# An attention and feed-forward kernel: x's layer norm and both its half-precision parts move to earlier stages, the router and the weights' pieces to later ones

## Chip, cores and metric

One Trainium2 chip, and of it one core. The metric is the device time of one launch in microseconds (us), the median of several runs.

## What is computed

The reference takes x (16 sequences, 256 channels, 1024 positions, float32) and a context y (16 x 256 x 512). Cut to what matters:

```python
xn = layernorm(x)                              # over the 1024 positions
q = ws(wq) @ y + bq;  k = ws(wk) @ y + bk      # ws: rows of the weights standardised
v = ws(wv) @ xn + bv
s = softmax(q @ k.T / SCALE)                   # 8 heads, 32 x 32 each
o = ws(wo) @ (s @ v) + bo + xn                 # then a norm over channels, gamma, beta, mask
x = x + tanh(g_xattn) * norm(o)
xr = layernorm(x).reshape(4096, 1024)          # tokens are the channels' rows
gates = top-2 of softmax(xr @ wr.T)            # 8 experts
h = silu(xr @ w1.T);  h = silu(h @ w3.T);  h = h @ w2.T
out = zeros; out[index of expert k] += gates[:, k] * h      # rows 0 to 7 only
x = x + tanh(g_ffn) * out
```

## The kernel before

Every float32 product is made of half-precision parts: a tensor is split into a high part (float16) and a low part (what the high one left out), and three products hi x hi, hi x lo, lo x hi are summed.

The 16 sequences go in 8 **pairs** (q = 2j and 2j + 1 for pair j; b is the place in the pair, 0 or 1). A pair's feed-forward part has 16 **groups** (g = 0 to 15): in each, TensorE makes eight steps (d = 0 to 7) of three products 128x128 by 128x512 (`ffn`, L665). Groups 0 to 7 multiply by w1, groups 8 to 15 by w3. In the same program order stand the 15 **stages** of the next pair's attention: stage s is mixed into group s + 1 of the pair before it. So pair j's feed-forward runs with pair j + 1's attention, and the kernel is one prologue (pair 0's attention and the split of the weights), eight pairs, and a short end. Groups and stages are written by hand in the same order on every engine; each engine has its own queue, runs it strictly in order, and waits on semaphores. What stands behind a waiting instruction waits too.

TensorE fills banks of PSUM. For a group g: ScalarE takes tanh (L899, `th_ready`), VectorE finishes the activation (L1344), ScalarE writes its high part (L905, `h_hi`), VectorE its low part (L1349, `h_lo`). Group g + 2 of TensorE needs L1344 of group g.

The steps of the attention that the text speaks of, by stage:

- Stages 0 and 2: four `project` products each (L539) on TensorE, emptied by VectorE (`qk_out`, L1292) and scaled by ScalarE (`q_scaled`, L842).
- Stages 1 and 3: `scores` (L548); VectorE's `softmax` (L1202 to L1218) with ScalarE's exponential (`score_exp`, L847) in its middle.
- Stages 3 and 4, d = 4: `out_times_scores` (L558). ScalarE writes its high part (`t1_high`, L858), VectorE its low part (`t1_low`, L1297).
- Stage 4, d = 0 and stage 5, d = 2: `times_value` (L573, L580), which needs `t1_low`. ScalarE empties it with `m_high` (L851 and, for cb, L854), VectorE with `m_low` (L1191). For b = 1, `out_times_scores` waits for the cb of b = 0 (`cb_evac`), since both use one bank.
- x's first norm: VectorE's statistics (`ln1`, L1176 and L1182), GpSimd's coefficients (`coefs`, L369 to L381, into `co`), ScalarE's `normed` (L793, writes xs), VectorE's high part (`x_high`, L1187), GpSimd's low part (`x_low`, L396). Stages 3 to 6.
- GpSimd's `bias_part` (L432) writes a part of the tile u, to which VectorE's `bias_tiles` (L1227) adds the rest.
- Stages 7 and 8, one per d: `long_product` (L595, L599), which needs x's high and low part; VectorE adds it to u (`attention_out`, L1243 and L1247, with statistics) and from its fifth tile on TensorE waits for VectorE to have emptied the bank.
- GpSimd's `add_beta` (L412, L415) and `values` (coefficients from the statistics of u); ScalarE's `v_normed` (L864); then TensorE's `attention_back` (L612) in stages 9 and 10.

The router (64 small products, L674, then `top_two` and `gates` on VectorE) is placed by three group numbers: its products behind group ROUTER[0], `top_two` behind group ROUTER[1], `gates` ahead of the activation of group ROUTER[2]. Its result is first needed in group 10.

In pair 0 the weights are still being split: a piece i (0 to 7 of w1, 8 to 15 of w3) is `w_high` on ScalarE (L831), `w_low` on VectorE (L1156) and two transposing DMAs from SyncE's queue (`turn`, L293). The pieces pass through five slots of buffers, and a slot is free when its last piece is turned. Group 8 of pair 0 needs all pieces of w3. In the tables below, names of buffers have their numbers left out (t_hi is t1_hi; h_hi and h_lo are also the slots of the weights' pieces).

Of the kernel before, what the change touches and what calls it, by code (L numbers as in the profile page):

```python
# [59 lines left out]
ROUTER = (1, 2, 3)  # L60
# [7 lines left out]
def build(nc, a, out):  # L68
# [14 lines left out]
    def w_slot(i):  # L83

        return ((3, 0), (4, 0), (0, 0), (1, 0), (2, 0), (0, 1), (1, 1), (2, 1),
                (0, 2), (1, 2), (2, 2), (0, 3), (1, 3), (2, 3), (0, 4), (0, 5))[i]

    def w_blocks(g):

        return {0: (5, 6, 7), 1: (8, 9), 2: (10, 11), 3: (12, 13), 4: (14,), 6: (15,)}.get(g, ())  # L90
# [5 lines left out]
    with ctx:  # L96
# [70 lines left out]
        co = sb("co", [P, 4, 2])  # L167
# [48 lines left out]
            mcur_set ln1_stat ln1_mv ln1_var ln1_rstd ln1_coef xs_ready xhi_ready xlo_ready mtmp_step xpre_ready  # L216
# [39 lines left out]
        def _(sp):  # L256
# [39 lines left out]
            def pair(j, last=False):  # L296

                load_x(j)
                if j == 1:
                    for i in range(FT, 2 * FT):  # L300
                        turn(i)
                if not last:
                    for b in range(2):
                        load_y(j + 1, b)
                store(j)
                for b in range(2):
                    tokens(j, b)
                if not last:
                    for b in range(2):
                        load_mask(j + 1, b)  # L310
# [18 lines left out]
            for i in range(2, FT):  # L329
                turn(i)  # L330
# [17 lines left out]
        def _(pool):  # L348
# [40 lines left out]
            def ln1(q):  # L389
                coefs(q, mv, co, CH, EPS, XS, "ln1", (sm["xs_ready"], q))  # L390

            def x_low(q, b):
                pool.wait_ge(sm["xhi_ready"], q + 1)
                for h in range(4):
                    n, at = h // 2, slice(TC * (h % 2), TC * (h % 2) + TC)
                    ins = pool.tensor_tensor(x_lo[:, b, n, at], xs[b][:, n, at], x_hi[:, b, n, at], ALU.subtract)  # L396
                ins.then_inc(sm["xlo_ready"], 1)
# [38 lines left out]
            def attention(j, s, jn=None):  # L436
                if s == 12 and jn is not None:
                    y_largest(jn)
                if s in (3, 4):
                    ln1(2 * j + s - 3)  # L440
                if s in (2, 3):
                    bias_part(2 * j + s - 2, s - 2)
                if s in (5, 6):
                    x_low(2 * j + s - 5, s - 5)
                if s == 7:
                    add_beta(j, 0, 0)
                    values(2 * j, 0)
                    add_beta(j, 0, 1)
                    add_beta(j, 1, 0)
                if s == 8:  # L450
                    values(2 * j + 1, 1)
                    add_beta(j, 1, 1)
                if s in (9, 10):
                    second_norm(2 * j + s - 9)
# [4 lines left out]
            ln1(0)  # L459
            x_low(0, 0)  # L460
            ln1(1)
# [18 lines left out]
        def _(pe):  # L480
# [154 lines left out]
            def ffn(j, g, d):  # L635
# [18 lines left out]
                else:  # L654
                    if g == FT:
                        pe.wait_ge(sm["h_lo"], GROUPS * j + d + 1)
                    if g == FT and d == 0 and first_pair(j):
                        for slot, n in enumerate((6, 4, 4)):
                            pe.wait_ge(w_turned[slot], 32 * n)
# [129 lines left out]
        def _(act):  # L789
            def normed(q, b, c_, s_coef, s_done):  # L790
                act.wait_ge(s_coef, q + 1)
                for c in range(CH):
                    ins = act.activation(xs[b][:, c, :], xa[b][:, c, :], ACT.Identity,  # L793
                                         bias=c_[:, 3, c:c + 1], scale=c_[:, 2, c:c + 1])
                ins.then_inc(s_done, 1)
# [93 lines left out]
            def attention_late(j, s, jn=None):  # L889
# [3 lines left out]
                if s in (4, 5):  # L893
                    normed(2 * j + s - 4, s - 4, co, sm["ln1_coef"], sm["xs_ready"])
# [17 lines left out]
            def group(j, g, ja=None, w3=False, jn=None):  # L912
                if ja is not None and g > 0:
                    attention(ja, g - 1)
                if w3:
                    for i in w_blocks(g):
                        w_high(i)
                    if g in (0, 2, 4, 6, FT):
                        n = (0, 2, 4, 6, FT).index(g)
                        act.wait_ge(w_turned[(3, 4, 1, 2, 0)[n]], (32, 32, 128, 128, 192)[n])  # L920
                    if g == FT:
                        act.wait_ge(sm["fs_set"], 2)
                ffn(j, g)
                if ja is not None:
# [17 lines left out]

            def x_high(b):

                act.wait_ge(sm["qk_mm"], CT * (b + 1))
                act.wait_ge(sm["xs_ready"], b + 1)
                act.activation(x_hi[:, b], xs[b], ACT.Copy).then_inc(sm["xhi_ready"], 1)
# [21 lines left out]
            normed(0, 0, co, sm["ln1_coef"], sm["xs_ready"])  # L969
            x_high(0)  # L970
            m_high(0, 0)
            score_exp(1)
            normed(1, 1, co, sm["ln1_coef"], sm["xs_ready"])
            t1_high(1, bk=rbk)
            x_high(1)
# [34 lines left out]
        def _(dve):  # L1010
# [174 lines left out]
            def x_high(q, b):  # L1185
                dve.wait_ge(sm["xs_ready"], q + 1)
                dve.tensor_copy(x_hi[:, b], xs[b]).then_inc(sm["xhi_ready"], 1)  # L1187

# [118 lines left out]
            def attention(j, s):  # L1307
# [3 lines left out]
                if s in (1, 3):  # L1311
                    softmax(2 * j + s // 2, s // 2)
                if s == 4:
                    m_low(2 * j, 0)
                if s in (3, 4):
                    t1_low(2 * j + s - 3)
                    ln1(j, s - 3)
                if s in (5, 6):
                    bias_tiles(2 * j + s - 5, s - 5)
                    x_high(2 * j + s - 5, s - 5)  # L1320
# [78 lines left out]
            def group(j, g, ja=None, w3=False, jn=None):  # L1399
                if ja is not None and g > 0:  # L1400
                    attention(ja, g - 1)
                if g == ROUTER[2]:
                    gates(j)
                if w3:
                    for i in w_blocks(g):
                        w_low(i)
                ffn(j, g)
# [138 lines left out]
```

## Time and profile before

| what | before |
|---|---|
| median of 3 runs | 1136.14 us (1135.68 to 1138.17) |
| profiled execution, its own time | 1137.7 us |
| its span, first to last instruction | 1135.8 us |
| busy in the span | PE 92%, DVE 71%, ACT 41%, POOL 37% |
| mean granted TensorE clock | 0.974 |
| first `ffn` product of pair 0 starts | 115.08 us |
| GpSimd, steady: four of L432, four of L396 | 4.04 us, 4.95 to 5.13 us |
| router's 64 products, pair 2: first starts, next other product starts | 402.32 us, 403.93 us |
| VectorE, pair 0: two of `w_low` (L1156) | 2.48 us |
| ScalarE: one of `w_high` (L831), mean | 1.14 us |
| pair 0, pairs 1 to 5: from the first `ffn` product to the next pair's | 144.03 us, 127.47 us |
| last piece of the weights: first transpose issued, second landed behind its issue | 191.83 us, 3.1 us |

PE is TensorE, DVE VectorE, ACT ScalarE, POOL GpSimd, SP SyncE (SPq its queue of DMAs). A row of the timeline has start, duration, engine, line, operation, output<-inputs, shapes, count of merged instructions, and in brackets the idle time ahead of it with what ended it.

### The profile page before, as it was taken

How to read it: one execution, taken by the hardware profiler on the slowest of the kernel's cores; microseconds unless marked ns; L12 is line 12 of the kernel's file. 1: busy time of each engine (PE TensorE's matmuls, PEld its weight loads, DVE VectorE, ACT ScalarE, POOL GpSimd, SP SyncE). 2: the span in 40 equal slices, each digit the busy share in tenths (PEclk: the TensorE clock that was granted, in tenths of full speed). 3: DMA queues.
4: the chain of work that ended last, by engine and by line, in shares of the span. 5: the costliest groups of instructions: out<-in, count | busy, mean ns of one | idle time of the engine just before them, and what ended most of it. 6: DMA issues, size and time to landing. Idle time of an engine off the chain costs nothing.

```text
span 1135.8 us, 17656 instructions
## 1 busy us (share of the span) xinstructions
PE 1043.5 (92%) x6502; PEld 594.8 (52%) x6502; DVE 805.0 (71%) x1915; ACT 469.9 (41%) x714; POOL 415.6 (37%) x498
## 2 busy tenths in 40 slices
PE   4672898999999999999999999999999999999998
PEld 2461454645555455645555455645555455644452
DVE  5987688975798668975798668975798668963221
ACT  4378344263335424263335424263336424262341
POOL 2493015831267014831267014831167015820000
PEclk9786889999999999999999999999999999999999
DMA  8705983153002700153002600162002600063000
GB/s 306 193 20 107 217 205 46 38 147 114 1 20 87 191 0 0 37 149 109 0 18 92 185 0 0 37 157 101 0 18 97 181 0 0 0 166 132 1 1 2
DMA packets 129377, 90.20 MB, mean 79 GB/s; under 512 B 103135, under 2 KB 112933, under 8 KB 129341
## 3 DMA queue, kind: packets, MB, share of 16 engines
q1 hardware_dynamic: 127280, 88.16, 28.1%
q10 hardware_dynamic: 2060, 1.58, 0.5%
q8 instruction: 20, 0.33, 0.1%
q14 instruction: 17, 0.13, 0.0%
HBM read 47.75 MB, written 16.81 MB: 57 GB/s over the span
## 4 chain that ended last, share of the span: by engine, by line
PE 55%; DVE 21%; POOL 9%; ACT 6%; issue 6%; DMA 2%; SPq 1%; POOLq 0%; ACTq 0%; DVEq 0%
PE bank L665 39%; PE bank L539 6%; DVE ub L1227 5%; POOL xbuf L415 3%; POOL mtmp L412 3%; POOL coc L376 2%; DVE ub L1247 2%; PE bank L548 2%; DVE bst L1176 2%; DVE ub L1243 2%; ACT ub L864 2%; PE bank L612 1%; ACT h_hi L905 1%; DVE x_hi L1187 1%; DVE act_t L1344 1%
## 5 line engine op out<-in xcount | busy, mean ns | idle before, releaser
L665 PE MATMUL bank<-xt_hi,w1b 128*128 128x512 f16 x1024 | 326.4, 381 | 1.8 <-DMA xt_lo<-mrow 1.2
L665 PE MATMUL bank<-w3b,h_hi 128*128 128x512 f16 x1024 | 304.5, 379 | 0.0
L665 PE MATMUL bank<-xt_lo,w1b 128*128 128x512 f16 x512 | 194.9, 381 | 0.0
L665 PE MATMUL bank<-w3b,h_lo 128*128 128x512 f16 x512 | 194.0, 379 | 0.0
L899 ACT ACTIVATE act_t<-bank,fs 128x512 f32<-128x512 f32 x128 | 86.9, 679 | 191.3 <-PE bank L665 191.3
L1349 DVE SCALAR_TENSOR_TENSOR h_lo<-act_t,h_hi 128x512 f16<-128x512 f32 x128 | 98.8, 772 | 91.7 <-ACT h_hi L905 91.7
L665 PEld LDWEIGHTS bank<-xt_hi,w1b 128*128 128x128 f16 x1024 | 100.5, 98 | 116.9 <-issue 3.7
L905 ACT ACTIVATE h_hi<-act_t 128x512 f16<-128x512 f32 x128 | 80.8, 631 | 193.8 <-DVE act_t L1344 193.8
L1344 DVE SCALAR_TENSOR_TENSOR act_t<-act_t,bank 128x512 f32<-128x512 f32 x128 | 86.6, 676 | 100.6 <-ACT act_t L899 100.3
L665 PEld LDWEIGHTS bank<-w3b,h_hi 128*128 128x128 f16 x1024 | 98.0, 98 | 76.0
L432 POOL TENSOR_TENSOR ub<-bo_b,mcur 128x512 f32<-128x512 f32 x64 | 65.4, 1051 | 189.7 <-DVE dg L1202 176.9
L369 POOL TENSOR_TENSOR co<-mv,minus 128x2 f32<-128x2 f32 x32 | 10.1, 316 | 227.6 <-DVE mv L1182 146.4
L396 POOL TENSOR_TENSOR x_lo<-xbuf,x_hi 128x512 f16<-128x512 f32 x64 | 80.6, 1290 | 32.1 <-DVE x_hi L1187 27.5
L539 PE MATMUL bank<-wqk_hi,x_hi 128*128 128x512 f16 x256 | 86.7, 384 | 0.5 <-DVE x_hi L1050 0.5
L415 POOL TENSOR_TENSOR xbuf<-xbuf,mtmp 128x512 f32<-128x512 f32 x64 | 81.7, 1276 | 5.0
L665 PEld LDWEIGHTS bank<-w3b,h_lo 128*128 128x128 f16 x512 | 50.0, 98 | 60.5
L864 ACT ACTIVATE ub<-ub,coc 128x256 f32<-128x256 f32 x128 | 64.7, 589 | 38.8 <-POOL coc L381 38.8
L665 PEld LDWEIGHTS bank<-xt_lo,w1b 128*128 128x128 f16 x512 | 50.3, 98 | 55.0 <-issue 0.6
L1292 DVE SCALAR_TENSOR_TENSOR ub<-bank,ysc,qkb_b 128x512 f32<-128x512 f32 x64 | 46.6, 748 | 44.8 <-PE bank L539 44.8
L599 PE MATMUL bank<-m_hi,x_hi 128*128 128x256 f16 x256 | 71.2, 278 | 0.0
L599 PE MATMUL bank<-m_lo,x_hi 128*128 128x256 f16 x256 | 71.0, 277 | 0.0
L599 PE MATMUL bank<-m_hi,x_lo 128*128 128x256 f16 x256 | 70.8, 277 | 0.0
(197 smaller groups left out, 1792.8 us busy)
## 6 DMA issues: line engine op xcount, KB each, us to landing
xbuf<-in_x_dram SPq DMA_DIRECT2D x16, 1024.0 KB, 8.7
out_dram<-xbuf SPq DMA_DIRECT2D x16, 1024.0 KB, 4.4
x_lo<-in_ctx_dram SPq DMA_DIRECT2D x16, 512.0 KB, 3.4
mrow<-in_mask_dram SPq DMA_DIRECT2D x16, 512.0 KB, 4.5
w1b<-in_w_dram SPq DMA_DIRECT2D x8, 512.0 KB, 6.7
w3b<-in_w_dram SPq DMA_DIRECT2D x8, 512.0 KB, 7.8
xbuf<-in_w_dram SPq DMA_DIRECT2D x1, 4096.0 KB, 13.7
xt_hi<-x_hi SPq DMA_TRANSPOSE x32, 3.4
```

The source lines that it names most:

```text
L396: ins = pool.tensor_tensor(x_lo[:, b, n, at], xs[b][:, n, at], x_hi[:, b, n, at], ALU.subtract)
L415: pool.tensor_tensor(xa[b][:, c, h], xa[b][:, c, h], mtmp[:, :], ALU.add)\
L432: ins = pool.tensor_tensor(u[b][:, tt, :], bo_b[:, :].unsqueeze(1).broadcast_to([P, 2, S]), m1c[:, b, tt].unsqueeze(2).broadcast_to([P, 2, ...
L539: mm = pe.matmul(bk[t][:, :], left[b][:, c, P * t:P * t + P], right[:, c, :], start=n == 0, stop=n == 5)
L599: mm = pe.matmul(bk[:, S:2 * S], left[:, b, c, P * t:P * t + P], right[:, b, c, :], start=n == 0, stop=n == 5)
L665: mm = pe.matmul(bk[:, :], left, right, start=d == 0 and n == 0, stop=d == FT - 1 and n == 2)
L864: act.activation(u[b][:, t, :], u[b][:, t, :], ACT.Identity, bias=coc[:, 3, t:t + 1], scale=coc[:, 2, t:t + 1]).then_inc(sm["v_ready"], 1)
L899: act.activation(act_t[:, g % 2, :], fbk[g % 2][:, :], ACT.Tanh, scale=fs[:, 0:1] if first else fs[:, 1:2]).then_inc(sm["th_ready"], 1)
L905: act.activation(h1_hi[:, g, :] if first else h2_hi[:, g % 3, :], act_t[:, g % 2, :], ACT.Copy, scale=H1S if first else H2S).then_inc(sm[" ...
L1227: ins = dve.scalar_tensor_tensor(out=u[b][:, t, :], in0=cb[:, b, :], scalar=m2c[:, b, t:t + 1], in1=u[b][:, t, :], op0=ALU.mult, op1=ALU.add)
L1344: dve.scalar_tensor_tensor(out=buf, in0=buf, scalar=1.0, in1=fbk[g % 2][:, :], op0=ALU.add, op1=ALU.mult)\
L1349: dve.scalar_tensor_tensor(out=lo, in0=buf, scalar=H1S if first else H2S, in1=hi, op0=ALU.mult, op1=ALU.subtract).then_inc(sm["h_lo"], 1)
```

## The change

The statistics of x move from stages 3 and 4 to stages 1 and 2; `normed` moves from stages 4 and 5 to 2 and 3 and writes both the high part and xs from x itself (four activations of 128x1024 for a sequence in place of two, and no `x_high` on VectorE). `co` has a copy for each b. On GpSimd `bias_part` of b = 0, both `ln1` and both `x_low` come in stages 2 and 3; `add_beta` waits until both bias tiles are made, and its fourth one stands ahead of `values` of b = 1. The router goes from groups 1, 2, 3 to 4, 5, 6. In pair 0 the weights' pieces are spread over more groups and stand behind a group's activation, where they stood ahead of it; their slots, the counts waited for and the order of SyncE's queue change with that.

```diff
@@ -57,7 +57,7 @@
-ROUTER = (1, 2, 3)
+ROUTER = (4, 5, 6)
@@ -83,11 +83,11 @@
         return ((3, 0), (4, 0), (0, 0), (1, 0), (2, 0), (0, 1), (1, 1), (2, 1),
-                (0, 2), (1, 2), (2, 2), (0, 3), (1, 3), (2, 3), (0, 4), (0, 5))[i]
+                (0, 2), (1, 2), (0, 3), (2, 2), (0, 4), (2, 3), (0, 5), (0, 6))[i]
...
-        return {0: (5, 6, 7), 1: (8, 9), 2: (10, 11), 3: (12, 13), 4: (14,), 6: (15,)}.get(g, ())
+        return {0: (5,), 1: (6,), 2: (7, 8), 3: (9, 10), 4: (11, 12), 5: (13, 14), 6: (15,)}.get(g, ())
@@ -164,7 +164,7 @@
         mvc = sb("mvc", [P, 8, 2])
-        co = sb("co", [P, 4, 2])
+        co = sb("co", [P, 2, 4, 2])
@@ -295,10 +295,11 @@
-                load_x(j)
                 if j == 1:
-                    for i in range(FT, 2 * FT):
+                    for i in range(FT - 2, 2 * FT):
                         turn(i)
+                else:
+                    load_x(j)
@@ -326,7 +327,10 @@
             store(0)
-            for i in range(2, FT):
+            for i in range(2, 4):
+                turn(i)
+            load_x(1)
+            for i in range(4, FT - 2):
@@ -386,11 +390,11 @@
-            def ln1(q):
-                coefs(q, mv, co, CH, EPS, XS, "ln1", (sm["xs_ready"], q))
+            def ln1(q, b):
+                coefs(q, mv, co[:, b], CH, EPS, XS, "ln1", (sm["xs_ready"], q - 1))
...
             def x_low(q, b):
-                pool.wait_ge(sm["xhi_ready"], q + 1)
+                pool.wait_ge(sm["xs_ready"], q + 1)
@@ -436,29 +440,34 @@
                     y_largest(jn)
-                if s in (3, 4):
-                    ln1(2 * j + s - 3)
-                if s in (2, 3):
-                    bias_part(2 * j + s - 2, s - 2)
-                if s in (5, 6):
-                    x_low(2 * j + s - 5, s - 5)
-                if s == 7:
+                if s == 2:
+                    pool.wait_ge(sm["s_ready"], 2 * j + 1)
+                    bias_part(2 * j, 0)
+                    ln1(2 * j, 0)
+                    ln1(2 * j + 1, 1)
+                if s == 3:
+                    x_low(2 * j, 0)
+                    bias_part(2 * j + 1, 1)
+                    x_low(2 * j + 1, 1)
+                if s == 6:
+                    pool.wait_ge(sm["ub_ready"], 2 * j + 2)
                     add_beta(j, 0, 0)
-                    values(2 * j, 0)
                     add_beta(j, 0, 1)
                     add_beta(j, 1, 0)
+                if s == 7:
+                    values(2 * j, 0)
+                    add_beta(j, 1, 1)
                 if s == 8:
                     values(2 * j + 1, 1)
-                    add_beta(j, 1, 1)
...
             bias_part(0, 0)
-            ln1(0)
+            ln1(0, 0)
             x_low(0, 0)
-            ln1(1)
+            ln1(1, 1)
@@ -655,7 +664,7 @@
                     if g == FT and d == 0 and first_pair(j):
-                        for slot, n in enumerate((6, 4, 4)):
+                        for slot, n in enumerate((7, 3, 4)):
@@ -787,12 +796,16 @@
         def _(act):
-            def normed(q, b, c_, s_coef, s_done):
-                act.wait_ge(s_coef, q + 1)
+            def normed(q, b):
+
+                act.wait_ge(sm["ln1_coef"], q + 1)
+                if isinstance(q, int) and q < 2:
+                    act.wait_ge(sm["qk_mm"], CT * (q + 1))
                 for c in range(CH):
-                    ins = act.activation(xs[b][:, c, :], xa[b][:, c, :], ACT.Identity,
-                                         bias=c_[:, 3, c:c + 1], scale=c_[:, 2, c:c + 1])
-                ins.then_inc(s_done, 1)
+                    for x in (x_hi[:, b], xs[b]):
+                        ins = act.activation(x[:, c, :], xa[b][:, c, :], ACT.Identity, bias=co[:, b, 3, c:c + 1],
+                                             scale=co[:, b, 2, c:c + 1])
+                ins.then_inc(sm["xs_ready"], 1)
@@ -890,8 +903,8 @@
                     y_high(jn, s - 13)
-                if s in (4, 5):
-                    normed(2 * j + s - 4, s - 4, co, sm["ln1_coef"], sm["xs_ready"])
+                if s in (2, 3):
+                    normed(2 * j + s - 2, s - 2)
@@ -913,14 +926,15 @@
                 if w3:
-                    for i in w_blocks(g):
-                        w_high(i)
                     if g in (0, 2, 4, 6, FT):
                         n = (0, 2, 4, 6, FT).index(g)
-                        act.wait_ge(w_turned[(3, 4, 1, 2, 0)[n]], (32, 32, 128, 128, 192)[n])
+                        act.wait_ge(w_turned[(3, 4, 1, 2, 0)[n]], (32, 32, 96, 128, 224)[n])
...
                 ffn(j, g)
+                if w3:
+                    for i in w_blocks(g):
+                        w_high(i)
@@ -939,12 +953,6 @@
                                    accum_out=wsum[:, k, f:f + 1]).then_inc(sm["w_rows"], 1)
-
-            def x_high(b):
-
-                act.wait_ge(sm["qk_mm"], CT * (b + 1))
-                act.wait_ge(sm["xs_ready"], b + 1)
-                act.activation(x_hi[:, b], xs[b], ACT.Copy).then_inc(sm["xhi_ready"], 1)
@@ -966,13 +974,11 @@
             small_high()
-            normed(0, 0, co, sm["ln1_coef"], sm["xs_ready"])
-            x_high(0)
+            normed(0, 0)
             m_high(0, 0)
             score_exp(1)
-            normed(1, 1, co, sm["ln1_coef"], sm["xs_ready"])
             t1_high(1, bk=rbk)
-            x_high(1)
+            normed(1, 1)
@@ -1182,10 +1188,6 @@
-            def x_high(q, b):
-                dve.wait_ge(sm["xs_ready"], q + 1)
-                dve.tensor_copy(x_hi[:, b], xs[b]).then_inc(sm["xhi_ready"], 1)
-
@@ -1310,14 +1312,14 @@
                     softmax(2 * j + s // 2, s // 2)
+                if s in (1, 2):
+                    ln1(j, s - 1)
...
                     t1_low(2 * j + s - 3)
-                    ln1(j, s - 3)
                 if s in (5, 6):
                     bias_tiles(2 * j + s - 5, s - 5)
-                    x_high(2 * j + s - 5, s - 5)
@@ -1401,10 +1403,10 @@
                     gates(j)
+                ffn(j, g)
...
                         w_low(i)
-                ffn(j, g)
```

The names of the removed semaphore `xhi_ready` and of its declaration are left out above.

ScalarE, the last two pairs (the attention of pair 7), from the scaling of the projections of b = 1 to the emptying of `times_value` of b = 0. Before:

```order
L842 ACTIVATE ub<-ub,mcur 128x256 x4
L899 ACTIVATE act_t<-bank,fs 128x512
L905 ACTIVATE h_hi<-act_t 128x512
L847 ACTIVATE dg<-dg 128x64
L858 ACTIVATE t_hi<-bank 128x512
L899 ACTIVATE act_t<-bank,fs 128x512
L905 ACTIVATE h_hi<-act_t 128x512
L851 ACTIVATE m_hi<-bank 128x512
L854 ACTIVATE cb<-bank,fs 128x256
```

The same place after the change, with the new line numbers (L806 is `normed`, L860 `score_exp`, L871 `t1_high`, L864 and L867 `m_high`):

```order
L918 ACTIVATE h_hi<-act_t 128x512
L806 ACTIVATE x_hi<-xbuf,co 128x1024
L806 ACTIVATE xbuf<-xbuf,co 128x1024
L806 ACTIVATE x_hi<-xbuf,co 128x1024
L806 ACTIVATE xbuf<-xbuf,co 128x1024
L860 ACTIVATE dg<-dg 128x64
L871 ACTIVATE t_hi<-bank 128x512
L912 ACTIVATE act_t<-bank,fs 128x512
L918 ACTIVATE h_hi<-act_t 128x512
L806 ACTIVATE x_hi<-xbuf,co 128x1024
L806 ACTIVATE xbuf<-xbuf,co 128x1024
L806 ACTIVATE x_hi<-xbuf,co 128x1024
```

Four activations of the norm now stand between h_hi and the exponential, and four more (three are shown) between the next h_hi and m_hi.

VectorE at the same place, from the end of one softmax to the next. Before, after the router's last row:

```order
L1396 TENSOR_TENSOR gts<-e1t,gts 128x4x8
L1344 SCALAR_TENSOR_TENSOR act_t<-act_t,bank 128x512
L1349 SCALAR_TENSOR_TENSOR h_lo<-act_t,h_hi 128x512
L1202 COPY dg<-bank 32x64 x4
L1205 TENSOR_REDUCE dr<-dg 128x2
L1207 TENSOR_TENSOR dg<-dg,dr 128x64
L1212 TENSOR_REDUCE dr<-dg 128x2
L1214 RECIPROCAL dr<-dr 128x2
L1218 TENSOR_TENSOR sblk<-dg,dr 32x2x32 x4
L1297 SCALAR_TENSOR_TENSOR t_lo<-bank,t_hi 128x512
L1176 BN_STATS bst<-xbuf 128x6 x4
```

And after the change (L1182 the statistics, L1346 and L1351 the activation of the group, L1220 the softmax's last products, L1299 `t1_low`):

```order
L1294 SCALAR_TENSOR_TENSOR ub<-bank,ysc,qkb_b 128x512 x4
L1182 BN_STATS bst<-xbuf 128x6 x4
L1019 MEMSET spare 128x1
L1188 BN_AGGR mv<-bst 128x2 x2
L1346 SCALAR_TENSOR_TENSOR act_t<-act_t,bank 128x512
L1351 SCALAR_TENSOR_TENSOR h_lo<-act_t,h_hi 128x512
L1204 COPY dg<-bank 32x64 x4
L1207 TENSOR_REDUCE dr<-dg 128x2
L1209 TENSOR_TENSOR dg<-dg,dr 128x64
L1214 TENSOR_REDUCE dr<-dg 128x2
L1216 RECIPROCAL dr<-dr 128x2
L1220 TENSOR_TENSOR sblk<-dg,dr 32x2x32 x4
```

The statistics, which stood behind `t1_low`, now stand ahead of the group's activation, where the router's gates stood.

ScalarE in pair 0, groups 6 and 7, around the last piece of the weights. Before:

```order
L793 ACTIVATE xbuf<-xbuf,co 128x1024 x2
L851 ACTIVATE m_hi<-bank 128x512
L854 ACTIVATE cb<-bank,fs 128x256
L831 ACTIVATE h_hi<-w3b,sc 128x1024
L899 ACTIVATE act_t<-bank,fs 128x512
L905 ACTIVATE h_hi<-act_t 128x512
```

After (L844 is `w_high`):

```order
L864 ACTIVATE m_hi<-bank 128x512
L867 ACTIVATE cb<-bank,fs 128x256
L912 ACTIVATE act_t<-bank,fs 128x512
L918 ACTIVATE h_hi<-act_t 128x512
L844 ACTIVATE h_hi<-w3b,sc 128x1024
L912 ACTIVATE act_t<-bank,fs 128x512
```

The last piece went from ahead of group 6's activation to behind it.

## Rows read from the trace of the kernel before

**Rows 1.** Page, busy us and share of the span

```profile
PE 1043.5 (92%) x6502; PEld 594.8 (52%) x6502; DVE 805.0 (71%) x1915; ACT 469.9 (41%) x714; POOL 415.6 (37%) x498
```

**Rows 2.** Timeline of PE, pair 2's three idle places (groups 7, 8, 10)

```profile
450.87 0.44 PE L595 MATMUL bank<-ident,xbuf 128*128 128x128 f32 x2 [0.84 <-POOL x_lo L396]
...
458.42 0.44 PE L595 MATMUL bank<-ident,xbuf 128*128 128x128 f32 x2 [1.24 <-DVE ub L1247]
...
485.12 0.65 PE L612 MATMUL bank<-ident,ub 128*128 128x128 f32 x4 [1.12 <-ACT ub L864]
```

**Rows 3.** Timeline of PE, pair 2, stage 4

```profile
429.27 0.27 PE L573 MATMUL bank<-t_hi,wv_hi 128*128 128x256 f16 x1
...
431.24 0.38 PE L665 MATMUL bank<-xt_hi,w1b 128*128 128x512 f16 x1
...
434.02 1.10 PE L558 MATMUL bank<-wo_t,sblk 128*128 128x256 f32 x4
```

**Rows 4.** Timeline of DVE, pair 2, group 4

```profile
421.00 0.75 DVE L1292 SCALAR_TENSOR_TENSOR ub<-bank,ysc,qkb_b 128x512 f32<-128x512 f32 x1 [1.19 <-PE bank L539]
...
427.02 0.22 DVE L1212 TENSOR_REDUCE dr<-dg 128x2 f32<-128x64 f32 x1 [0.32 <-ACT dg L847]
...
427.48 0.91 DVE L1218 TENSOR_TENSOR sblk<-dg,dr 32x64 f32<-32x64 f32 x4
428.42 0.69 DVE L1297 SCALAR_TENSOR_TENSOR t_lo<-bank,t_hi 128x512 f16<-128x512 f32 x1
429.03 2.46 DVE L1176 BATCH_NORM_STATS2 bst<-xbuf 128x6 f32<-128x512 f32 x4
...
431.72 0.64 DVE L1344 SCALAR_TENSOR_TENSOR act_t<-act_t,bank 128x512 f32<-128x512 f32 x1
```

**Rows 5.** Timeline of ACT, pair 2, groups 4 to 6

```profile
426.74 0.26 ACT L847 ACTIVATE dg<-dg 128x64 f32<-128x64 f32 x1 [2.10 <-DVE dg L1207]
...
432.39 0.63 ACT L905 ACTIVATE h_hi<-act_t 128x512 f16<-128x512 f32 x1 [2.23 <-DVE act_t L1344]
432.93 0.58 ACT L851 ACTIVATE m_hi<-bank 128x512 f16<-128x512 f32 x1
433.41 0.47 ACT L854 ACTIVATE cb<-bank,fs 128x256 f32<-128x256 f32 x1
...
440.30 2.36 ACT L793 ACTIVATE xbuf<-xbuf,co 128x1024 f32<-128x1024 f32 x2
442.56 0.57 ACT L851 ACTIVATE m_hi<-bank 128x512 f16<-128x512 f32 x1
```

**Rows 6.** Timeline of POOL in the prologue

```profile
48.87 4.51 POOL L396 TENSOR_TENSOR x_lo<-xbuf,x_hi 128x512 f16<-128x512 f32 x4 [4.60 <-ACT x_hi L947]
```

**Rows 7.** Timeline of DVE in the same stretch of the prologue

```profile
50.37 3.33 DVE L1218 TENSOR_TENSOR sblk<-dg,dr 32x64 f32<-32x64 f32 x4
```

**Rows 8.** Timeline of DVE, pair 2, group 10

```profile
478.02 0.54 DVE L1256 BATCH_NORM_AGGREGATE mvc<-bst 128x2 f32<-128x6 f32 x7
```

**Rows 9.** Timeline of POOL, pair 2, group 10

```profile
479.60 0.20 POOL L369 TENSOR_TENSOR coc<-mvc,minus 128x8 f32<-128x8 f32 x1
```

**Rows 10.** Timeline of PE, pair 0, groups 2 and 4

```profile
140.26 3.78 PE L548 MATMUL bank<-ub 128*128 128x128 f32 x16 [3.32 <-ACT ub L842]
...
162.55 3.53 PE L548 MATMUL bank<-ub 128*128 128x128 f32 x16 [2.04 <-ACT ub L842]
```

**Rows 11.** Windows: busy us by engine, PEclk is the granted clock

```profile
139.00:145.70 6.70, 5.44 (x21) 4.27 (x22) 4.39 (x7) 4.30 (x6) 0.00 (x0) 0.50 0.96 269
...
162.90:166.20 3.30, 3.30 (x17) 3.06 (x16) 3.20 (x6) 2.25 (x3) 0.00 (x0) 0.50 0.03 7
115.08:259.11 144.03, 131.54 (x786) 74.88 (x787) 112.45 (x252) 62.41 (x89) 53.12 (x60) 0.95 0.58 131
386.58:514.05 127.47, 124.22 (x802) 71.08 (x799) 96.06 (x229) 52.07 (x80) 51.29 (x60) 1.00 0.23 65
```

**Rows 12.** Timeline of SyncE's queue, the last piece's second transpose

```profile
193.10 1.34 SPq L293 DMA_TRANSPOSE w3b<-h_lo  x1
```

More of the change, by code:

```diff
@@ L215, in build @@
             mask_tr mask_copy mask_sq tg_set gcol_set bias_set fs_part fs_set
-            mcur_set ln1_stat ln1_mv ln1_var ln1_rstd ln1_coef xs_ready xhi_ready xlo_ready mtmp_step xpre_ready
+            mcur_set ln1_stat ln1_mv ln1_var ln1_rstd ln1_coef xs_ready xlo_ready mtmp_step xpre_ready
             y_max y_col y_top y_row y_all y_clamp y_bits y_scale y_hi_set y_split
```

## The prediction

> **What bounds the kernel now.** The page's first part shows TensorE busy for 92% of the span and the next engine for 71% [rows 1]: the end is set by TensorE's work plus its idle time, so I looked for TensorE's waits, then for what the change does to each chain that ends in one. The windows by pair come next: a steady pair takes 127.47 us, 124.22 of them busy, at clock 1.00; pair 0 takes 144.03 at 0.95 [rows 11]. In the timeline a steady pair waits at three places: 0.84 us for x_lo, 1.24 for VectorE to empty a long product, 1.12 for v_normed [rows 2]. One more 0.2 is lost ahead of out_times_scores (below). A wait costs some 0.16 more than its bracket, since the last product ahead of it is drawn 0.38 long and the next would have started 0.22 after it; so the three are worth 1.0, 1.4 and 1.3. In pair 0, TensorE waits 3.32 and 2.04 us for q_scaled and runs at clock 0.50 behind both [rows 10, 11].
>
> **A steady pair, the exponential.** Times are pair 2's. The fourth qk_out of b = 1 starts at 421.00 and takes 0.75, so VectorE is free at 421.67 (starts overlap a little) [rows 4]. The statistics of x take 2.69 (429.03 to 431.72) and now stand ahead of group 3's activation, which thus starts at 424.36. h_hi follows 0.67 later (431.72 to 432.39) and the next thing on ScalarE 0.54 after that [rows 4, 5]: 425.57. There now stand four activations of the norm. Two took 2.26 from start to next start (440.30 to 442.56), so four take 4.52 and the exponential starts at 430.09; before, it started at 426.74 [rows 5]. L1212 follows 0.28 later, L1218 another 0.46 [rows 4, 5]: 430.83.
>
> **The collision.** x_low of b = 0 on GpSimd, which worked in stage 5, now starts when the norm is written, at 430.09 + 0.2 (the last activation's end): 430.3, just ahead of L1218. In the prologue the same meeting can be read: x_low runs from 48.87 for 4.51 [rows 6] and the four L1218 beside it take 3.33 [rows 7]; alone they take 0.91 [rows 4]. Each of the four seems to wait for a GpSimd instruction to end. Here they start with the first, and GpSimd has four, so I take their end at that of x_low, 434.8; the bounds are 431.7 (no collision) and 434.8. The Trainium skill, page "SBUF — State Buffer", section "SBUF: two separate sides", says that VectorE and GpSimd share a pair of ports that one of them holds for a whole instruction. By that rule, the trace's 3.33 beside 0.91 is what is to be expected.
>
> Then t1_low, 0.69, ends at 435.55, and times_value starts at 435.6. It is due at 429.27 + 1.61 for the router's products, which now stand ahead of it (402.32 to 403.93 in the table), 430.88 [rows 3]. TensorE waits 4.7; without the collision 1.7.
>
> **The second wait.** VectorE starts group 4's activation at 435.47, h_hi 436.14, and now four activations of b = 1 stand ahead of m_high: 436.68 + 4.52 = 441.20. L854 starts 0.48 behind it and takes 0.47 [rows 5]: 442.15, and out_times_scores 0.14 later (433.88 to 434.02), 442.3 [rows 3, 5]. TensorE itself would come there at 435.6 + 1.97 + 2.60 = 440.2 (429.27 to 431.24 to 434.02, less the 0.18 that it waits now) plus what the clock costs. After waits of 3.32 and 2.04 it ran at 0.50 for 5.4 and 3.3 busy us, which costs 2.7 and 1.65 [rows 10, 11]; waits up to 1.24 left it at 1.00 [rows 2, 11]. So I add 1.65 to 2.7: 441.9 to 442.9. Whichever ends last, 442.3 to 442.9; undisturbed it would be 434.02 − 0.18 + 1.61 = 435.45. The delay is 6.8 to 7.5; I take 7.2, and less the 0.2 lost there now it is 7.0. The Trainium skill, page "TensorE: Matmul & The Clock Gate", section "What's actually happening", says that idleness halves the clock and activity restores it; the rows of pair 0 agree, and a wait of 4.7 lies above both of theirs.
>
> **What a steady pair gains.** x_low is done long before stage 7: 1.0 [rows 2]. At group 8, VectorE no longer casts x_high, but takes over top_two and gates in groups 5 and 6; between nothing of that wait and all of it, 0.6 to 1.4, I take 1.0. At group 10 add_beta no longer stands ahead of values of b = 0, nor the fourth ahead of the coefficients: they started at 479.60, while the statistics end at 478.56 [rows 8, 9]. That is 1.0 earlier, and v_normed with it: 1.1 of the 1.3, or all with the group's 0.2 that is left. I take 1.4 with it. Sum 3.4, between 2.6 and 3.9. Net 7.0 − 3.4 = +3.6; six pairs (1 to 6): **+21.6**.
>
> **Pair 0.** It takes 16.6 more than a steady pair [rows 11], whose own waits are 4.3; of these 20.9, 18.8 lie where the change reaches: the two waits for q_scaled with their clock (3.32 + 2.04 + 2.7 + 1.65 and 0.75 for small ones, 10.5), and the same places as in a steady pair, each longer, since the weights' pieces stand ahead (8.3). Pieces and activations change places, so I count all 18.8 as gone. New: (1) times_value. Two w_high (2.28) and two w_low (2.48) lie in the same chain, in parallel for most of it: 4.7 + 2.7 = 7.4, and 2.7 for the clock. (2) out_times_scores 1.5 more. (3) The last piece. VectorE starts group 6's activation 5.8 us after group 7 begins on TensorE (my estimate, by laying its rows of groups 5 and 6 in the new order); w_high can start 1.2 later, takes 1.14, w_low 1.24 to 2, and its two transposes land 4.4 after it (issue at 191.83 and 193.10, 3.1 to landing) [rows 12]: 14.1 after the start of group 7. Group 8, which needs it, is due at 6.1. A wait of 7.7 to 8, and 2.7 for the clock. Before, the piece had landed at 196.2, ahead of need. (4) 1.0 for the others. Together 23.3: **+4.5**.
>
> **Elsewhere.** In the prologue four activations (4.52) stand for two and a cast (4.27) on ScalarE: +0.5. The loads of x for pair 1 go later in SyncE's queue and land some 3 us ahead of need: nothing; if late, up to 3. Costed at nothing: top_two and gates (3.4 of VectorE) lie beside groups 5 and 6, without that cover they would be 3.4 a pair; bias_part earlier waits for a softmax, with nothing but x_low behind it; ScalarE's 2.26 more a sequence is hidden outside these chains by its 59% idle [rows 1].
>
> Sum: 1137.7 (profiled execution) + 21.6 + 4.5 + 0.5 = 1164.3. The profiled execution lies 1.6 above the median, so the median comes to **1162.5**.
>
> **Rivals.**
> (a) The forecast, 0.60; its own range 1152 to 1174. Low end: the gains 3.9 and a delay of 6.8 (−5.4), or piece 15's wait hidden (−10.5, because VectorE comes to it earlier). High end: 2.7 at both clocks, and a third of a half-clock stretch after the second wait (+1.65 for each pair).
> (b) No collision, 0.20: VectorE gets its turns between GpSimd's as the small operands suggest; the 2.42 lost in the prologue over four instructions speaks against it. times_value waits 1.7, under the 2.04 that halved the clock, and cb is done 3.0 earlier: the delay is 3.8, the net +0.2 to +1.2 with the gains 3.6 to 2.6; pair 0 about +1.5. Time 1139 to 1149, centre 1142.
> (c) Slower by more than (a), above 1174, 0.06: x of pair 1 or the bias tiles late too.
> (d) Faster, 0.10: the norm's activations in pairs read the same data and take half, 0.57 each, where they took 1.13. Both chains then lose 2.26 and the delay is 6.85 − 4.5 = 2.35, under the gain of 3.4: −1.05 × 6, pair 0 about −1: 1129. It decides from 0.70 us an activation down. Against it: w_high, with a half-precision output of the same size, takes 1.14.
> (e) The change cancels out within 0.2% (2.3 us, about what a measurement of this kernel can tell from none), 0.04: (b) with its full gains.
>
> **Range.** From 1138.5, which takes in (b), to 1174; out of it lie (c), (d) and (e), 0.2 together. Faster 0.10 is (d), same 0.04 is (e), slower 0.86 is (a), (b) and (c).
>
> **What the changed profile would show.** If right: in every pair TensorE idle for 4 to 5 us ahead of times_value of b = 0, ended by VectorE's t_lo; the four L1220 (as they are then) near 4 us beside GpSimd's x_lo; PEclk 0.50 for some us behind; perhaps a short idle time for cb ahead of out_times_scores; the three idle places of [rows 2] shorter or gone; pairs 131 us long. In pair 0 no idle time ahead of the scores, and one of some 8 ahead of group 8, ended by a DMA on w3b. Wrong if: L1220 takes 0.9 (rival b); the exponential starts less than 4 us behind the norm's first activation (d); the wait at times_value leaves the clock at 1.00, which takes 10 to 16 off the total without changing its sign.

## The result, and the profile after

The changed kernel takes 1160.2 us (1159.53 to 1161.12, 4 runs), the kernel before 1136.25 in the same comparison: ratio 1.021, 95% interval 1.0197 to 1.0222. The forecast was 1162.5 with a range of 1138.5 to 1174.

The page after, first the busy times of the engines with their shares of the span, then TensorE's line of the 40 slices and the granted clock:

```profile
PE 1050.1 (91%) x6502; PEld 599.5 (52%) x6502; DVE 784.8 (68%) x1901; ACT 499.7 (43%) x744; POOL 400.9 (35%) x498
...
PE   4571976999899998999899998999899998999998
...
PEclk9886989999899998999899998999899998999999
```

Beside [rows 1]: the same TensorE instructions, busy for 6.6 us more, which is the half clock. VectorE has 20 us less to do and ScalarE 30 more, and neither is near being full. The rest is waiting. Windows of the stretch behind times_value in pair 2, of pair 0 and of pair 2 (start:end, length, busy us of the five engines, granted clock, DMA share, GB/s):

```profile
440.14:443.66 3.52, 3.52 (x18) 2.55 (x19) 1.98 (x2) 2.95 (x4) 3.52 (x4) 0.54 0.00 0
...
115.71:262.38 146.67, 130.08 (x785) 73.33 (x786) 110.38 (x250) 66.98 (x93) 49.62 (x60) 0.93 0.55 129
392.69:523.00 130.31, 125.28 (x802) 72.06 (x800) 92.80 (x227) 56.27 (x84) 49.36 (x60) 0.97 0.22 63
```

A steady pair takes 130.31 us where it took 127.47, pair 0 takes 146.67 where it took 144.03 [rows 11]. Pairs 1 to 6 together are 18.8 longer, pair 0 2.6, the prologue 0.6: 22.0, and the span grew by 22.0. All of what TensorE waits for in pair 2 (waited for, us in total, times, longest):

```profile
PE bank L582 <- DVE t_lo L1299: 4.6, 1, 4.6
PE bank L567 <- ACT cb L867: 0.4, 1, 0.4
```

The three places of [rows 2] are gone, and times_value (L582) has taken over. Pair 2's chain into it, from the timeline of the changed kernel, ScalarE first:

```profile
429.54 0.63 ACT L918 ACTIVATE h_hi<-act_t 128x512 f16<-128x512 f32 x1 [2.16 <-DVE act_t L1346]
430.08 1.23 ACT L806 ACTIVATE x_hi<-xbuf,co 128x1024 f16<-128x1024 f32 x1
431.21 1.23 ACT L806 ACTIVATE xbuf<-xbuf,co 128x1024 f32<-128x1024 f32 x1
432.35 1.23 ACT L806 ACTIVATE x_hi<-xbuf,co 128x1024 f16<-128x1024 f32 x1
433.48 1.23 ACT L806 ACTIVATE xbuf<-xbuf,co 128x1024 f32<-128x1024 f32 x1
434.61 0.24 ACT L860 ACTIVATE dg<-dg 128x64 f32<-128x64 f32 x1
...
446.25 0.46 ACT L867 ACTIVATE cb<-bank,fs 128x256 f32<-128x256 f32 x1
```

GpSimd and VectorE behind it, and TensorE:

```profile
434.78 4.49 POOL L400 TENSOR_TENSOR x_lo<-xbuf,x_hi 128x512 f16<-128x512 f32 x4 [3.83 <-ACT xbuf L806]
```

```profile
435.34 4.02 DVE L1220 TENSOR_TENSOR sblk<-dg,dr 32x64 f32<-32x64 f32 x4
439.39 0.69 DVE L1299 SCALAR_TENSOR_TENSOR t_lo<-bank,t_hi 128x512 f16<-128x512 f32 x1
440.00 0.68 DVE L1346 SCALAR_TENSOR_TENSOR act_t<-act_t,bank 128x512 f32<-128x512 f32 x1
```

```profile
440.14 0.39 PE L582 MATMUL bank<-t_hi,wv_hi 128*128 128x256 f16 x1 [4.60 <-DVE t_lo L1299]
...
446.85 1.10 PE L567 MATMUL bank<-wo_t,sblk 128*128 128x256 f32 x4 [0.43 <-ACT cb L867]
```

The reader is to see four things: the exponential (L860) directly behind four activations of the norm; x_low (L400) starting 0.56 ahead of the four L1220; these taking 4.02 where [rows 4] have 0.91, and ending just behind GpSimd's fourth; and TensorE at 0.54 of its clock from the wait's end to the start of the next group.

In pair 0 the waits for q_scaled [rows 10] are nearly gone (0.40 at L557). These came instead, from the timeline of TensorE:

```profile
168.25 0.39 PE L582 MATMUL bank<-t_hi,wv_hi 128*128 128x256 f16 x1 [6.96 <-DVE t_lo L1299]
...
177.05 0.46 PE L567 MATMUL bank<-wo_t,sblk 128*128 128x256 f32 x1 [1.42 <-ACT cb L867]
...
201.75 0.58 PE L674 MATMUL bank<-w3b,h_hi 128*128 128x512 f16 x1 [7.82 <-DVE act_t L1346]
```

and of SyncE's queue:

```profile
198.42 1.34 SPq L293 DMA_TRANSPOSE w3b<-h_lo  x1
```

The trace names L1346 as the releaser of group 8, but that ended 0.86 us before; the last transpose, issued at 198.42 and landed 3.1 later at 201.5, is nearer: 0.2 ahead of group 8. Experiment e8 asks which it was.

### The profile page after: what moved, and what is told of

Same layout as the page of the kernel before. It is cut to its first block, busy times and chain, and to the rows that moved or that the text cites. A ratio compares the mean times of both kernels' runs of the same rounds, so it can differ in the third digit from the quotient of the medians.

```text
span 1157.9 us, 17670 instructions
## 1 busy us (share of the span) xinstructions
PE 1050.1 (91%) x6502; PEld 599.5 (52%) x6502; DVE 784.8 (68%) x1901; ACT 499.7 (43%) x744; POOL 400.9 (35%) x498
## 4 chain that ended last, share of the span: by engine, by line
PE 74%; DVE 10%; ACT 9%; POOL 3%; issue 2%; DMA 1%; ACTq 1%; SPq 0%; DVEq 0%; POOLq 0%
PE bank L674 50%; PE bank L548 6%; PE bank L608 6%; DVE sblk L1220 2%; ACT x_hi L806 2%; PE bank L621 2%; ACT xbuf L806 2%; PE bank L604 2%; DVE bst L1182 2%; PE bank L582 1%; PE bank L731 1%; DVE ub L1229 1%; PE bank L557 1%; PE bank L698 1%; DVE act_t L1346 1%
## 5 line engine op out<-in xcount | busy, mean ns | idle before, releaser
L1351 DVE SCALAR_TENSOR_TENSOR h_lo<-act_t,h_hi 128x512 f16<-128x512 f32 x128 | 96.9, 757 | 91.5 <-ACT h_hi L918 91.5
L1346 DVE SCALAR_TENSOR_TENSOR act_t<-act_t,bank 128x512 f32<-128x512 f32 x128 | 86.6, 677 | 106.3 <-ACT act_t L912 105.3
L436 POOL TENSOR_TENSOR ub<-bo_b,mcur 128x512 f32<-128x512 f32 x64 | 68.1, 1096 | 191.5 <-DVE sblk L1220 177.8
L416 POOL TENSOR_TENSOR mtmp<-mrow,gcol 128x512 f32<-128x512 f32 x64 | 68.9, 1077 | 118.0 <-DVE ub L1229 113.7
L400 POOL TENSOR_TENSOR x_lo<-xbuf,x_hi 128x512 f16<-128x512 f32 x64 | 71.9, 1156 | 52.2 <-ACT xbuf L806 52.2
L419 POOL TENSOR_TENSOR xbuf<-xbuf,mtmp 128x512 f32<-128x512 f32 x64 | 84.4, 1318 | 5.0
L855 ACT ACTIVATE ub<-ub,mcur 128x256 f32<-128x256 f32 x64 | 32.5, 508 | 92.4 <-DVE ub L1294 91.7
```

What stands on the lines that cost most here:

```text
L416: pool.tensor_tensor(mtmp[:, :], mrow[:, b, h], gcol[:, 1, c:c + 1].broadcast_to([P, TC]), ALU.mult)\
L419: pool.tensor_tensor(xa[b][:, c, h], xa[b][:, c, h], mtmp[:, :], ALU.add)\
L436: ins = pool.tensor_tensor(u[b][:, tt, :], bo_b[:, :].unsqueeze(1).broadcast_to([P, 2, S]), m1c[:, b, tt].unsqueeze(2).broadcast_to([P, 2, ...
L1346: dve.scalar_tensor_tensor(out=buf, in0=buf, scalar=1.0, in1=fbk[g % 2][:, :], op0=ALU.add, op1=ALU.mult)\
L1351: dve.scalar_tensor_tensor(out=lo, in0=buf, scalar=H1S if first else H2S, in1=hi, op0=ALU.mult, op1=ALU.subtract).then_inc(sm["h_lo"], 1)
```

## The experiments

Theory: the four norm activations ahead of the exponential, and x_low beside L1220, make TensorE wait at times_value; the norm of b = 1 ahead of cb makes a second chain. Rivals: the router's move is what costs; the four L1220 are slow for another reason; only the clock costs; the late last piece is not what group 8 of pair 0 waits for. All ratios are to the kernel before, with 95% intervals. The edits are to the changed kernel unless said. The copies differ in line numbers by one or two, so L583 is L582 and so on.

**e1, GpSimd's x_low of b = 0 behind the softmax of b = 1.**

```diff
                 if s == 3:
+                    pool.wait_ge(sm["s_ready"], 2 * j + 2)
                     x_low(2 * j, 0)
```

> The changed kernel with one more wait: GpSimd starts x_low of b = 0 only when the softmax of b = 1 is done. Theory: VectorE's four L1220 wait for GpSimd's instructions. Then they take 0.9 us in place of 4.0, t1_low ends 3.1 earlier, TensorE waits 1.5 ahead of times_value in place of 4.6, its clock stays at 1.00 there, and the second wait, for cb, grows from 0.4 to some 2, since its chain (activation, h_hi, four norm activations) is only 3.1 earlier: 3.8 lost in place of 7.0, pairs of 127.1 us in place of 130.3, total near 1138. Rival, the four are slow for another reason (ScalarE beside them, or their shape): 4 us again, total 1160. Rival, only the clock costs: the gain stays under 2 us a pair, total 1148 or more.

Measured: 1140.02 us, ratio 1.0041 (1.0028 to 1.0053). Timelines of VectorE and TensorE in pair 2:

```profile
431.12 0.91 DVE L1221 TENSOR_TENSOR sblk<-dg,dr 32x64 f32<-32x64 f32 x4
```

```profile
432.80 0.28 PE L583 MATMUL bank<-t_hi,wv_hi 128*128 128x256 f16 x1 [1.48 <-DVE t_lo L1300]
...
439.52 0.46 PE L568 MATMUL bank<-wo_t,sblk 128*128 128x256 f32 x1 [0.32 <-ACT cb L868]
```

L1220 falls to 0.91, the first wait to 1.48, steady pairs to 127.20. So the collision, by itself, is worth 20 of the 24 us. One point missed: in four of the six steady pairs the clock still fell behind the wait of 1.48 or 1.49. In pair 2 it was 0.58 in the 3.2 us behind it, and the second wait was only 0.32; in pair 1 the clock stayed at 1.00 and the second wait was 1.99. Both pairs took 127.20: cb's chain sets the end, whatever the clock does ahead of it.

**e2, x_low in eight instructions of half the size** (`for h in range(8)` over 256 columns each).

> The changed kernel with x_low in eight GpSimd instructions of half the size. If each L1220 waits for the end of one running GpSimd instruction, the four take about 4 x 0.6 = 2.4 us in place of 4.0, t1_low comes 1.6 earlier, a pair gains 1.6, total near 1149. If VectorE waits for all of x_low, or the sharing is by bandwidth, the four take 4 us or more still, and the total is 1160 to 1163.

Measured: 1148.77 us, ratio 1.0113 (1.0096 to 1.013). VectorE and GpSimd:

```profile
433.81 2.08 DVE L1220 TENSOR_TENSOR sblk<-dg,dr 32x64 f32<-32x64 f32 x4
```

```profile
433.25 5.07 POOL L400 TENSOR_TENSOR x_lo<-xbuf,x_hi 128x256 f16<-128x256 f32 x8 [3.83 <-ACT xbuf L806]
```

GpSimd is busy for longer (5.07) and the four L1220 take 2.08, about half of 4.02; TensorE's wait at times_value is 2.66. So each L1220 waits for one running GpSimd instruction to end, not for the whole operation. The Trainium skill, page "SBUF — State Buffer", section "SBUF: two separate sides", calls the shared ports an exclusive lock held for the whole instruction and not a split of bandwidth. The traces agree: 2.08 beside 4.02.

**e3, the router's move alone, on the kernel before** (`ROUTER = (4, 5, 6)` and nothing else).

> The kernel before with only the router's three group numbers changed to 4, 5, 6. Theory: TensorE has the same products; 0.2 lost ahead of out_times_scores goes (times_value starts later than needed), but top_two and gates now lie in groups 5 and 6 on VectorE, ahead of x_high, so the 0.84 wait for x_lo may grow by up to 1.5. Between -0.3 and +1.5 a pair: 1134 to 1147, middle 1139. Rival, the router's move is what costs the new 7 us: total above 1150.

Measured: 1173.36 us, ratio 1.0328 (1.0311 to 1.0345). My range was missed by 26 us, and the rival's number (above 1150) came out; whether the move costs in the changed kernel too is asked by e5. Pair 2, VectorE's gates and GpSimd's x_low, and TensorE:

```profile
456.44 0.73 DVE L1375 TENSOR_SCALAR gd<-gd 128x4 f32<-128x4 f32 x1
457.21 0.18 DVE L1377 RECIPROCAL gd<-gd 128x4 f32<-128x4 f32 x1
457.31 1.01 DVE L1380 TENSOR_TENSOR e1t<-iot,topf 128x32 f32<-128x32 f32 x1
458.24 1.19 DVE L1380 TENSOR_TENSOR e2t<-iot,topf 128x32 f32<-128x32 f32 x1
459.35 1.16 DVE L1384 TENSOR_TENSOR gd<-gd 128x4 f32<-128x4 f32 x1
```

```profile
456.00 4.49 POOL L396 TENSOR_TENSOR x_lo<-xbuf,x_hi 128x512 f16<-128x512 f32 x4 [2.74 <-DVE x_hi L1187]
```

```profile
460.54 0.44 PE L595 MATMUL bank<-ident,xbuf 128*128 128x128 f32 x2 [1.76 <-POOL x_lo L396]
...
471.65 0.69 PE L595 MATMUL bank<-ident,xbuf 128*128 128x128 f32 x2 [4.04 <-DVE ub L1247]
```

The same meeting at another place: gates start 0.44 us behind x_low, and four of their operations take 0.73 to 1.19 us in place of 0.16 to 0.19, 3.4 more in all; the activation behind them is late, and the fifth long product waits 4.04. How much of the 37 us is the meeting, and how much is only that top_two and gates stand there, no run takes apart. That the router's products are 1.6 us on TensorE in either place was right; I had not looked at what stands beside gates.

**e5, the changed kernel with the router back** at groups 1, 2, 3.

> The changed kernel with the router at groups 1, 2, 3 as before. The router alone made the kernel before 37 us slower, because there gates and x_low of b = 0 met in group 7. Theory: in the changed kernel x_low is gone from there, and the router's products cover 1.6 us of the wait ahead of times_value, while gates ahead of group 3's activation would put the exponential 1.6 us later. So the router back costs 3.2 us a pair, total near 1182. Rival, the router's move is what costs in the changed kernel too: total well below 1160.

Measured: 1179.43 us, ratio 1.0377 (1.036 to 1.0395), steady pairs 133.49. The wait ahead of times_value is 7.79. Both the wait and the pair are 3.2 longer than in the changed kernel, as expected. So the router's move costs 37 us in the kernel before and gives 19 in the changed one, where x_low is gone from stage 5 and the router's products fill part of the wait: the two parts of the change can't be judged apart from each other.

**e4, the weights' pieces as before**, with slots, counts and the queue's order.

> The changed kernel with the weights' pieces, their slots, counts and the order of SyncE's queue as they were. Theory: only pair 0 changes. The 8 us wait ahead of group 8 and the half clock behind it go (9.3), the wait ahead of times_value falls from 7.1 to about 4.7 (2.4), and the waits for q_scaled with their half clock come back (10). Pair 0 within 3 us of 146.7, total 1157 to 1162. Rival, the late last piece is not the cause of the wait ahead of group 8: it stays, and the total is 1168.

Measured: 1160.62 us, ratio 1.0218 (1.0201 to 1.0236), the same as the changed kernel. Pair 0 took 147.40. The waits for q_scaled come back (3.32 and 1.81), the 7.8 at group 8 falls to 2.59, and the wait at times_value did not fall as expected (7.27). The pieces' move is worth nothing either way.

**e8, the last piece ahead of group 6's activation**, `w_high(15)` on ScalarE and `w_low(15)` ahead of the gates on VectorE.

> The changed kernel with the weights' last piece ahead of group 6's activation, its w_low ahead of the router's gates. Theory: w_low ends at 193.1 in place of 197.0 and the second transpose lands 4.4 behind it, so the wait ahead of group 8 falls from 7.8 to some 4 and the total by 4, to 1156. Rival, VectorE's activation of group 6 or 7 is what group 8 waits for: no gain, 1160.

Measured: 1158.79 us, ratio 1.02 (1.0183 to 1.0217). Pair 0 is 145.25. Timelines of ScalarE, VectorE, TensorE and SyncE's queue in pair 0:

```profile
191.50 1.15 ACT L844 ACTIVATE h_hi<-w3b,sc 128x1024 f16<-128x1024 f32 x1 [3.94 <-DMA w3b<-h_lo]
```

```profile
192.68 1.28 DVE L1164 SCALAR_TENSOR_TENSOR h_lo<-w3b,sc,h_hi 128x1024 f16<-128x1024 f32 x1 [1.78 <-ACT h_hi L844]
```

```profile
198.62 0.58 PE L674 MATMUL bank<-w3b,h_hi 128*128 128x512 f16 x1 [5.69 <-issue]
```

```profile
195.26 1.34 SPq L293 DMA_TRANSPOSE w3b<-h_lo  x1
```

The wait falls by 2.1, not 4: counted from the start of group 7 the piece is 2.2 us earlier, and no more, because its slot is free only when the piece before it has been turned (ScalarE waits 3.94 us for that DMA). Issued at 195.26, the last transpose lands 3.1 later at 198.4, again 0.2 ahead of group 8, and so it does in e4 (204.1 and 204.29). VectorE's activation had ended at 196.17 in e8. So group 8 waits for the piece. Of the 2.1, pair 0 keeps only 1.4: the half clock behind the wait cost more here (group 8 took 14.34 in place of 13.45).

**e6, the statistics behind the group's activation** on VectorE.

```diff
-                if s in (1, 2):
-                    ln1(j, s - 1)
...
                 ffn(j, g)
+                if ja is not None and g in (2, 3):
+                    ln1(ja, g - 2)
```

> The changed kernel with x's statistics on VectorE behind the group's activation in place of ahead of it. If the activation's place alone sets the chain, everything is 2.7 us earlier and the total near 1141. Theory: the tanh of group 3 ends at 427.4, only 1.5 us ahead of where the activation starts now, and the statistics then stand ahead of the softmax, whose last operation ahead of the exponential ends at 433.5; the exponential starts 1.0 earlier, a pair gains 1.0, total near 1153.

Measured: 1154.69 us, ratio 1.0163 (1.0146 to 1.018), steady pairs 129.25: 1.05 less, as expected.

**e7, the norm of b = 1 behind m_high of b = 0** on ScalarE.

> The changed kernel with the norm of b = 1 behind m_high of b = 0 on ScalarE. Theory: the wait of 4.6 ahead of times_value and the half clock behind it stay, the wait of 0.4 ahead of out_times_scores goes: 0.5 a pair, total near 1156.5. Rival, the second wait is as large as the first: a pair gains 3 or more, total under 1140.

Measured: 1161.73 us, ratio 1.0226 (1.0209 to 1.0243): no gain, where 1156.5 was expected. In the changed kernel only two of the six steady pairs wait for cb noticeably (pair 2 for 0.43 us, pair 6 for 0.31); in the others TensorE at its half clock comes hardly earlier than cb. The wait is gone in pair 2, but x_low of b = 1 is later, and 0.1 to 1.1 is lost at group 8. The second chain is worth nothing as long as the first stands.

**e9, e8 + e7 + e1 together.**

> The changed kernel with three edits together: x_low of b = 0 behind the softmax of b = 1, the norm of b = 1 behind m_high of b = 0, the last piece ahead of group 6's activation. If the two waits are one chain each and in series, the first leaves 1.6 lost a pair, the second (2.2 in the first experiment) goes, and 0.7 comes at group 8, since x_low of b = 1 is late: pairs of 125.7 us, total near 1127. Rival, the norm's move alone was worth nothing and is worth nothing here: total 1138.

Measured: 1129.79 us, ratio 0.9941 (0.9923 to 0.9959), pairs of 126.11. With the first wait at 1.49, the norm's move pays what the first chain's repair exposed: 1.1 a pair.

**e11, these three and e6.**

> The kernel of the three edits together, and x's statistics behind the group's activation as well. In the experiment with the statistics alone the chain came 1.0 us earlier. Here too the wait of 1.6 ahead of times_value should fall to 0.6; group 8 keeps its 1.0. Pairs of 125.1 in place of 126.1, total near 1123. Rival, something else holds t1_low: total 1130.

Measured: 1122.2 us (1120.78 to 1123.2), ratio 0.9879 (0.9862 to 0.9895): the fastest of all. TensorE in pair 2, and the windows of pairs 1 and 2:

```profile
424.07 0.28 PE L583 MATMUL bank<-t_hi,wv_hi 128*128 128x256 f16 x1 [0.41 <-DVE t_lo L1304]
...
451.44 0.33 PE L605 MATMUL bank<-ident,xbuf 128*128 128x128 f32 x1 [0.78 <-DVE ub L1254]
```

```profile
255.77:380.81 125.04, 123.83 (x802) 71.24 (x799) 90.54 (x227) 56.31 (x84) 49.35 (x60) 1.00 0.24 68
380.81:505.86 125.05, 123.84 (x803) 71.24 (x801) 90.53 (x227) 56.13 (x84) 49.37 (x60) 1.00 0.23 67
```

**e10, the exponential and t1_high ahead of the norm** in both stages, and e8.

> The changed kernel with score_exp and t1_high ahead of the norm in stages 3 and 4 (the norm of b = 0 comes behind the exponential of b = 1, that of b = 1 behind m_high and t1_high), and the last piece ahead of group 6's activation. Theory: the exponential starts when VectorE's subtraction ends, 432.3 in the changed kernel's times, x_low starts only at 437.5 and meets no L1220, t1_low ends at 434.7, ahead of times_value at 435.5: no wait there, clock 1.00. A wait for cb of up to 0.6, and 0.7 at group 8 as in the run with the later norm. Pairs of 124 to 125 us, total 1112 to 1120, below the kernel before. Rival, ScalarE falls behind with the tanh of group 4 (4.5 late) and TensorE waits in group 6 or for cb: total 1130 or more.

Measured: 1144.5 us, ratio 1.007 (1.0052 to 1.0089): my range was missed by 24 us, and the steady pairs take 127.7 or 129.2. The first step came true, no wait at times_value in the steady pairs; the rival too, a few groups later than I had placed it: the tanh of group 5 came 2.6 us into group 6, TensorE waited 1.21 for the activation at group 8 and 2.01 for VectorE inside it.

**e12, the same with the norm of b = 1 split** around t1_high.

> The kernel with the exponential first and the last piece ahead, and the norm of b = 1 in two halves: two activations ahead of t1_high, two behind it. In the run with all four behind it, the tanh of group 5 came 2.6 us into group 6, and everything on VectorE after it was late: 3.6 lost at groups 7 and 8. If that tanh is the cause, it comes 1.2 earlier (as long as t1_high fits), and at least that much comes back at group 8, with the half clock behind the wait there: pairs of 125 to 127 in place of 127.7 to 129.2, total 1125 to 1137. Rival, x_low of b = 1 beside top_two is the cause: it starts 1.2 earlier too, but meets as much: no gain, 1144.

Measured: 1135.77 us, ratio 0.9991 (0.9982 to 1.0001). The tanh is 1.4 earlier and group 7's loss falls from 1.38 to 0.30, as expected of it; the steady pairs take 126.7 or 128.2. The wait inside group 8 stayed at 2.01. The traces say how it arises: VectorE's activation that group 8 needs ends 0.05 us ahead of group 8's start in both e10 and e12, and VectorE then comes to the long products by the same row of work, 6.4 us after that start; in e11, with a wait of 0.78, the activation ends 1.3 ahead and VectorE is there after 5.15. So VectorE's lateness is what is left. No run removes it alone, so only half of the theory is shown.

## Why the prediction was right, point by point

- **The exponential**: forecast 430.09, which is 9.09 behind the start of the fourth qk_out. In the changed trace that starts at 425.51 and the exponential at 434.61, 9.10 behind it.
- **The collision**: forecast 4.0 for L1220 (430.83 to 434.8), measured 4.02. e1 and e2 show it as the cause, by taking it away and by halving its grain.
- **The wait at times_value**: forecast 4.7, measured 4.60 [rows 3].
- **The clock**: a term that was mis-sized. I added 1.65 to 2.7. From times_value to the next group it took 3.52 where [rows 3] have 1.97, so it cost 1.55 in pair 2, and 1.85 in pair 1: near the low bound, and the high one was too dear.
- **The second wait and the delay**: forecast 7.0 net a pair. Groups 4 and 5 lose 6.96 over bare work (a group's length less that of the same products with no idle time at the full clock), against 0.25 before: 6.7.
- **The gains**: forecast 3.4. Groups 7, 8, 10 and 11 of pair 2, the three places of [rows 2] and the group behind the last, lost 4.1 over bare work and now lose 0.2: 3.9. The wait at group 8, of which I gave 1.0, is gone wholly (1.46). Net 2.8 a pair in place of 3.6: over six pairs 18.8 (pairs 3 and 6 are each 0.7 longer than the others) in place of 21.6.
- **Pair 0**: forecast +4.5, measured +2.6; times_value 6.96 (7.4), group 8 7.82 (7.7 to 8), out_times_scores 1.42 (1.5). The clock again cost less: 2.4 behind times_value and 1.3 behind group 8's wait, against 2.7 each. The 1.3 is in part chance: behind the same wait of 7.82 e1's group 8 took 14.69 in place of 13.45, a cost of 2.5.
- **Elsewhere**: prologue +0.63, forecast 0.5; x of pair 1 was not late.
- **The rivals**: no collision (b) is e1, which measured 1140, where 1142 was worked out; its premise that so short a wait leaves the clock alone failed in four pairs of six. (d) is excluded: the four activations are 1.13 apart. (a) held.
- **The total**: 1162.5 is 2.3 above what was measured, and that it is so near is partly luck. The additions were 26.6 (21.6 + 4.5 + 0.5) and the span grew by 22.0: 4.6 too much (2.8 too much in the six pairs and 1.9 in pair 0, 0.1 too little in the prologue). The sum then took off 1.6, by which the profiled execution of before lay above its median; the profiled execution of after (1159.74) lies 0.5 below its own. This closed 2.1 of the 4.6. And 1164.3 less 1.6 is 1162.7, not 1162.5.

## What to carry to other kernels

When an operation moves, ask of every engine what runs beside it at its new place: here the same x_low cost 3.1 us a pair more beside four tiny VectorE operations than behind them (e1), and in e3 it met the router's gates. Work on an in-order engine that moves ahead of a short link of a chain (an exponential of 0.24 us behind 4.5 us of norm) costs there what is left of it when the link could start, though the engine is idle for more than half of the time: in pair 2 VectorE had the exponential's input ready at 432.25, and it started at 434.61. Parts of a change must be tried together as well as apart: the router's move was worth +37 us alone and −19 in company, and moving the second norm gave nothing until the first wait was mended.

## What the runs showed of the hardware that was not expected

The granted clock did not follow the length of the wait alone. In e12, two pairs with the same wait of 2.01 us ahead of the same product went on at different clocks. Windows of 3 us behind the wait, pair 1 and pair 2:

```profile
330.20:333.20 3.00, 3.00 (x16) 1.99 (x17) 3.00 (x10) 0.00 (x0) 2.77 (x4) 0.65 0.00 0
458.40:461.40 3.00, 3.00 (x22) 2.24 (x23) 3.00 (x10) 0.00 (x0) 2.77 (x4) 1.00 0.00 0
```

In e1 a wait of 1.48 was enough in pair 2 and one of 1.49 was not in pair 1, while e4's wait of 2.59 ahead of group 8 and e12's of 3.03 in pair 6 left the clock at 1.00. From pair 0 on, waits of 4 and more were followed by the low clock in every run. What decides between is left open. And in e3 a VectorE operation with one input tensor in SBUF (L1375, 0.73 in place of 0.16) was held beside GpSimd too, not only those with two; the reciprocal behind it (L1377) took its usual 0.18 while GpSimd ran.
